# A gated linear scan over four batches: weight splits after a norm, other PSUM banks for two products, a third gate buffer

## The reference

```python
def _L0_attn_ref(x, W_in, conv_w, conv_b, W_g, b_g, forget_base, W_out):
    gx = jnp.einsum('ntd,hd->nth', x, W_in)
    gate, xb = (gx[..., :H], gx[..., H:])
    xb = _depthwise_causal_conv(xb, conv_w, conv_b)          # 4 taps along the tokens
    fg = jnp.einsum('nth,gh->ntg', xb, W_g) + b_g
    forget, inp = (fg[..., :H], fg[..., H:])
    alpha = jnp.exp(-8.0 * softplus(forget_base) * sigmoid(forget))
    beta = jnp.sqrt(1.0 - alpha ** 2 + 1e-6)
    h = _linear_scan(alpha, beta * sigmoid(inp) * xb)        # h[t] = alpha[t] h[t-1] + xs[t]
    return jnp.einsum('nth,dh->ntd', gelu(gate) * h, W_out)
x = x + _L0_attn_ref(_layernorm(x), ...)
```

## Time and profile before

| What | us |
|---|---|
| median of 3 timed runs (lowest, highest) | 990.32 (987.42, 992.02) |
| profiled execution, first to last instruction | 990.8 |
| PE busy, in the span | 924.9 (93%) |
| DVE, ACT, POOL busy | 675.9, 513.9, 422.6 |
| from the start to the end of the scan layer's pipeline on TensorE | about 131 |

### The profile page before, as it was taken

How to read it: one execution, slowest core, us unless ns; L and a number is a source line. 1 busy time by engine, 2 the same in 40 slices (tenths; PEclk the granted TensorE clock), 3 DMA queues, 4 the chain that set the end, 5 groups by cost and what they waited for, 6 DMA issues and landing times.

```text
span 990.8 us, 17519 instructions
## 1 busy us (share of the span) xinstructions
PE 924.9 (93%) x5688; PEld 774.2 (78%) x5688; DVE 675.9 (68%) x1706; ACT 513.9 (52%) x1221; POOL 422.6 (43%) x420
## 2 busy tenths in 40 slices
PE   5889996999999988999999899999999999889998
PEld 4668875787878866888888678887888888778887
DVE  6878797558687677677767555567766667735563
ACT  5467751313131426767666644454766666654443
POOL 5333354112221357767676400006776767631110
PEclk9889998999999999999999999999999999999999
DMA  7200123000000000000001030000000000000001
GB/s 261 70 1 16 48 65 112 1 1 0 0 0 1 1 23 1 2 23 0 22 0 33 12 105 15 4 25 2 2 24 0 22 0 12 27 15 17 31 25 46
DMA packets 15716, 26.34 MB, mean 27 GB/s; under 512 B 1642, under 2 KB 12256, under 8 KB 14896
## 3 DMA queue, kind: packets, MB, share of 16 engines
q1 hardware_dynamic: 15664, 25.69, 8.0%
HBM read 20.53 MB, written 2.10 MB: 23 GB/s over the span
## 4 chain that ended last, share of the span: by engine, by line
PE 72%; DVE 11%; ACT 6%; issue 3%; POOL 3%; SPq 3%; DMA 2%; ACTq 0%; DVEq 0%; POOLq 0%
PE bank L1593 33%; PE bank L1941 5%; PE bank L1895 5%; PE bank L1919 5%; PE bank L1801 5%; PE bank L1905 4%; ACT probs L1460 3%; PE bank L1764 2%; PE bank L1882 2%; PE bank L1747 1%; SPq L352 1%; DVE y L820 1%; PE bank L1929 1%; PE bank L2014 1%; PE bank L2011 1%
## 5 line engine op out<-in xcount | busy, mean ns | idle before, releaser
L1460 ACT ACTIVATE probs<-bank,row_min 128x256 f32<-128x256 f32 (+1 forms) x256 | 110.4, 458 | 120.1 <-DVE row_min L1048 120.1
L569 POOL TENSOR_TENSOR norms<-norms,minus_half 128x16 f32<-128x16 f32 x32 | 93.6, 2924 | 2.7
L1048 DVE CUSTOM_DVE_ANT_0 bank<-bank,mask 128x256 f32<-128x256 f32 (+1 forms) x256 | 90.7, 425 | 5.9 <-PE bank L1895 5.7
L1593 PE MATMUL bank<-wqkv_hi,x_hi 128*128 128x512 f32 x192 | 82.4, 429 | 1.8 <-DVE rot L1024 1.1
L1593 PE MATMUL bank<-wqkv_lo,x_hi 128*128 128x512 f32 x192 | 76.3, 397 | 0.0
L1593 PE MATMUL bank<-wqkv_hi,x_lo 128*128 128x512 f32 x192 | 75.7, 394 | 0.0
L1185 DVE SCALAR_TENSOR_TENSOR hidden<-bank,lcols,hidden 128x512 f32<-128x512 f32 (+1 forms) x48 | 36.0, 749 | 51.9 <-PE bank L1593 28.2
L551 POOL TENSOR_TENSOR q_tok<-rot 128x512 f32<-128x512 f32 x32 | 41.2, 1288 | 57.7 <-DVE rot L1024 57.7
L1905 PE MATMUL bank<-ident,probs 128*128 128x128 f32 x448 | 61.5, 279 | 3.9 <-ACT probs L1460 3.9
L1593 PE MATMUL bank<-t_hi,wm_hi 128*128 128x512 f32 x160 | 63.6, 397 | 0.0
L1593 PE MATMUL bank<-t_lo,wm_hi 128*128 128x512 f32 x160 | 63.5, 397 | 0.0
(11 more groups left out here) (253 smaller groups left out, 2639.5 us busy)
## 6 DMA issues: line engine op xcount, KB each, us to landing
w_stage<-in_wm_l_dram SPq DMA_DIRECT2D x8, 534.0 KB, 3.7
w_stage<-in_wqkv_dram SPq DMA_DIRECT2D x2, 1536.0 KB, 8.0
out_dram<-stream SPq DMA_DIRECT2D x8, 256.0 KB, 2.4
emb<-in_ctx_dram SPq DMA_DIRECT2D x1, 1536.0 KB, 6.8
inner<-in_w_gate_dram SPq DMA_DIRECT2D x1, 1152.0 KB, 10.3
stream<-in_x_dram SPq DMA_DIRECT2D x2, 512.0 KB, 5.7
stream<-in_x_dram SPq DMA_DIRECT2D x1, 1024.0 KB, 12.8
ew<-in_pos_bias_dram SPq DMA_DIRECT2D x1, 1024.0 KB, 11.5
```

The costliest lines, as they stand in the source:

```text
L569: pool.tensor_tensor(norms[:, 2, :], norms[:, 1, :], minus_half[:, :], ALU.pow).then_inc(c_rn, 1)
L1048: dve.tensor_tensor_reduce(logits, logits, mask[:, 2 * P - nk:2 * P], 1.0, FAR, ALU.add, ALU.min, row_min[:, w % 2, 2 * i + e:2 * i + e + ...
L1460: act.activation(probs[:, i, e, 0:nk], logits, ACT.Exp, bias=row_min[:, w % 2, h:h + 1], scale=-1.0, accum_out=row_sum[:, w % 2, h:h + 1]) ...
L1593: ins = pe.matmul(out, stationary, moving, start=(first and i == 0), stop=(last and i == len(terms) - 1))
```

## The change

Five edits, all in the scan layer.

- Gelu of batch 2 writes a third buffer, `gate_third`, which lies where later weights (`w_1_hi`) go; only batch 3 waits for a buffer, and that wait is for batch 0's products.
- Input products 5 and 6 of a batch go to banks 6 and 7, the output's. Their waits change with it: in batch 1 and 2 for Gelu of the batch before, in batch 3 for the residual of batch 0. The output waits for Gelu. The other four input products and all gate products go round banks 2 to 5, two banks further with each batch.
- On DVE, the residual of batch b - 1 stands in front of the scan of batch b (for b = 1 and 2), where it stood behind it.
- On GpSimd, batch 1's `rstd_of` stands directly after the first rounding of a gate weight, and the first subtraction waits until batch 1's norm has been applied; five of the six weight instructions then follow.
- On DVE, batch 1's norm is applied ahead of four small instructions on constants, and its `low_part` ahead of the second convolution instead of behind it.

```diff
@@ -131,6 +131,9 @@
         ew = sb("ew", [P, TT, T], stack=st_bias)
         st_bias.close()
         w_1_lo = sb("w_1_lo", [P, KD, FH], F32R, stack=st12)
+        st_third = ExitStack()
+        gate_third = sb("gate_third", [P, KR, T], stack=st_third)
+        st_third.close()
         w_1_hi = sb("w_1_hi", [P, KD, FH], F32R, stack=st12)
         w_2 = sb("w_2", [P, KF, D], stack=st12)
         rows = sb("rows", [P, 4, D], stack=st12)
@@ -259,6 +262,16 @@
         (a_in, x1_in) = signals("a_in x1_in")
         w_raw = inner[:, :, :].rearrange("p n d -> p (n d)")
 
+        gate_acts = (gate_act[:, 0, :, :], gate_act[:, 1, :, :], gate_third, gate_act[:, 0, :, :])
+
+        def input_bank(b, j):
+
+            return bank[2 + (j + 2 * max(b - 1, 0)) % 4] if j < 4 else bank[2 + j]
+
+        def gate_bank(b, u):
+
+            return bank[2 + (u + 2 * b) % 4]
+
         C_ZERO = 2
         tiles = lambda b: bass.ts(b, TT) if not isinstance(b, int) else slice(b * TT, (b + 1) * TT)
         block = ctx.enter_context(nc.Block())
@@ -424,17 +437,18 @@
                 pool.wait_ge(a_gelu, 3 * b + 3)
                 for j in range(KR):
                     pool.wait_ge(a_scan, 3 * b + j + 1)
-                    pool.tensor_tensor(scanned[:, j, :], scanned[:, j, :], gate_act[:, b % 2, j, :], ALU.mult)\
+                    pool.tensor_tensor(scanned[:, j, :], scanned[:, j, :], gate_acts[b][:, j, :], ALU.mult)\
                         .then_inc(a_gh, 1)
 
             pool.memset(beyond_raw[:, :], 0.0).then_inc(e_beyond, 1)
             rstd_of(0)
             pool.wait_ge(wg_in, 16)
             for k in range(KR):
-                if k == 1:
-                    rstd_of(1)
                 raw_k = w_raw[:, WIN_COLS + k * 2 * RH:WIN_COLS + (k + 1) * 2 * RH]
                 pool.tensor_scalar(w_gate_hi[:, k, :], raw_k, 1.0, 0.0, ALU.mult, ALU.add).then_inc(wg_hi, 1)
+                if k == 0:
+                    rstd_of(1)
+                    pool.wait_ge(n_norm, 2 * TT)
                 pool.wait_ge(wg_hi, k + 1)
                 pool.tensor_tensor(w_gate_lo[:, k, :], raw_k, w_gate_hi[:, k, :].bitcast(F32), ALU.subtract)\
                     .then_inc(wg_split, 1)
@@ -736,7 +750,9 @@
                 for j in range(KR):
                     dve.wait_ge(a_xs0, 3 * b + j + 1)
                     dve.tensor_tensor(th_in[:, j, :], th_in[:, j, :], beta[:, j, :], ALU.mult).then_inc(a_xs, 1)
-                if not (isinstance(b, int) and b == 0):
+                if 0 < b < NB - 1:
+                    residual(b - 1)
+                elif b:
                     dve.wait_ge(a_o, 2 * b)
                 for j in range(KR):
                     dve.wait_ge(a_xs, 3 * b + j + 1)
...
@@ -881,6 +897,7 @@
             dve.wait_ge(x1_in, 16)
             dve.wait_ge(a_tp, 2)
             norm_stats(1, 1)
+            norm_apply(1, 1, False)
             dve.wait_ge(col_in, 16)
             dve.tensor_scalar(fb_tmp[:, 2, :], cols[:, C_FB:C_FB + KR], 0.0, None, ALU.max).then_inc(fb_vec, 1)
             dve.tensor_scalar(half_bf[:, :], cols[:, C_BG:C_BG + 2 * KR], 0.5, None, ALU.mult).then_inc(fb_vec, 1)
@@ -889,10 +906,9 @@
             dve.tensor_tensor(fb_tmp[:, 2, :], fb_tmp[:, 2, :], fb_tmp[:, 0, :], ALU.add).then_inc(fb_vec, 1)
             dve.wait_ge(fb_vec, 3)
             dve.tensor_scalar(m4sp[:, :], fb_tmp[:, 2, :], -4.0, None, ALU.mult).then_inc(fb_vec, 1)
-            norm_apply(1, 1, False)
             conv_taps(0, 0)
+            low_part(1, a_tp_out, a_tp_lo)
             conv_taps(0, 1)
-            low_part(1, a_tp_out, a_tp_lo)
             conv_low(0, 0)
             conv_taps(0, 2)
             conv_low(0, 1)
@@ -921,9 +937,7 @@
                 for j in range(KR):
                     conv_low(b + 1, j)
                 recurrence(b)
-                if b:
-                    residual(b - 1)
-                else:
+                if b == 0:
                     largest_bias()
 
             for b in range(NB - 1):
...
@@ -1275,11 +1289,11 @@
 
             def gelu_gate(b):
 
-                if b > 1:
-                    act.wait_ge(a_gh, 3 * b - 3)
+                if b == NB - 1:
+                    act.wait_ge(a_gh, 3)
                 for j in range(KR):
                     act.wait_ge(a_in, 6 * b + KR + j + 1)
-                    act.activation(gate_act[:, b % 2, j, :], bank[2 + (KR + j) % 4][:, :], ACT.Gelu).then_inc(a_gelu, 1)
+                    act.activation(gate_acts[b][:, j, :], input_bank(b, KR + j)[:, :], ACT.Gelu).then_inc(a_gelu, 1)
 
 
             act.wait_ge(w1s_in, 16)
...
@@ -1608,17 +1622,17 @@
                 pe.wait_ge(a_tp_lo, 2 * b + 2)
                 for j in range(2 * KR):
                     m = (j + KR) % (2 * KR)
-                    if b == 1 and j < 2:
-                        pe.wait_ge(a_gelu, 2 + j)
-                    elif b == 1 and j < 4:
-                        pe.wait_ge((a_tap0, a_gelu)[j - 2], (3, 1)[j - 2])
+                    if b == 1:
+                        pe.wait_ge(a_tap0 if j < KR else a_gelu, j % KR + 1)
                     elif b and j < 4:
                         pe.wait_ge((a_thf, a_th)[j % 2], 3 * (b - 2) + (2 + j) // 2 + 1)
-                    if j >= 4:
-                        pe.wait_ge(a_tap0, 3 * b + j - 4 + 1)
+                    elif b == 2:
+                        pe.wait_ge(a_gelu, 3 + j - KR + 1)
+                    elif b:
+                        pe.wait_ge(a_res, 2 * (b - 3) + j - 4 + 1)
                     if b == 0 and j % KR == 0:
                         pe.wait_ge(win_lo, KD * (j // KR + 1))
-                    product(bank[2 + j % 4][:, :], [
+                    product(input_bank(b, j)[:, :], [
                         (w[:, k, m * P:(m + 1) * P], x[:, k, :]) for k in range(KD)
                         for w, x in ((w_in_hi, t_hi), (w_in_hi, t_lo), (w_in_lo, t_hi))]).then_inc(a_in, 1)
 
@@ -1629,11 +1643,11 @@
                         u = 2 * j + g
 
                         if b == NB - 1 and u < 4:
-                            pe.wait_ge((a_thf, a_th)[g], 3 * b - (0 if u < 2 else 1))
-                        elif u == 0:
-                            pe.wait_ge(a_tap0, 3 * (b + 1) + 3)
-                        elif u < 4:
-                            pe.wait_ge(a_gelu, 3 * (b + 1) + u)
+                            pe.wait_ge((a_thf, a_th)[g], 3 * b - (1 if u < 2 else 0))
+                        elif u < KR:
+                            pe.wait_ge(a_tap0, 3 * (b + 1) + u + 1)
+                        elif u == KR:
+                            pe.wait_ge(a_gelu, 3 * (b + 1) + 1)
                         elif u == 4:
                             pe.wait_ge(a_thf, 3 * b + 1)
                         else:
...
@@ -1653,6 +1667,7 @@
             def output(b):
 
                 pe.wait_ge(a_gh, 3 * b + 3)
+                pe.wait_ge(a_gelu, 3 * min(b + 3, NB))
                 pe.wait_ge(a_res, 2 * b)
                 for t in range(TT):
                     for k in range(KR):
```

More of the change, by code:

```diff
@@ L749, in recurrence @@
                     dve.wait_ge(a_scan, 3 * b + j + 1)
-                    dve.tensor_tensor(scanned[:, j, :], scanned[:, j, :], gate_act[:, b % 2, j, :], ALU.mult)\
+                    dve.tensor_tensor(scanned[:, j, :], scanned[:, j, :], gate_acts[b][:, j, :], ALU.mult)\
                         .then_inc(a_gh, 1)
@@ L1267, in taps @@
                 for j in range(KR):
-                    src = bank[2 + j % 4]
+                    src = input_bank(b, j)
                     act.wait_ge(a_in, 6 * b + j + 1)
@@ L1644, in gates @@
                                 pe.wait_ge(a_conv_lo, 3 * b + k + 1)
-                            ins = product(bank[2 + (u + 2) % 4][:, :], [
+                            ins = product(gate_bank(b, u)[:, :], [
                                 (w[:, k, m * P:(m + 1) * P], c[:, k, :])
```

4 lines of the change are left out of this document (2 added, 2 removed).

## The result

The changed kernel takes 981.59 us (median of 4 runs, 981.32 to 983.12) beside 991.17 of the kernel before in the same session; the ratio is 0.9915, 95% interval 0.9894 to 0.9936. Forecast were 986.8 us and a range of 982 to 990.5: the two medians lie 9.6 us apart (8.4 us by the ratio), not 3.5, and the time is 0.4 us under the lower end of the range. Run once more in another session it took 982.95 us (6 runs, 982.11 to 983.55), ratio 0.9924 [0.9904, 0.9945]. The profiled executions span 979.5 and 981.4 us, against 990.8.

What follows compares the result with a forecast made beforehand. TensorE was taken as the bound, through scan-layer waits and a slow clock. Banks and buffer 5.2 + first wait 1.1 - residual 0.8 - clock 2.0 = 3.5 us, from 990.32 to 986.8 us; range 982 to 990.5.

Steps and rivals of the forecast that it cites:

- What bounds it, and which waits go and come: TensorE bounds the kernel; its scan-layer waits go, a hidden 2.40 us norm wait appears, the rest moves as a block.
- The three waits: TensorE's waits: 4.8 us before batch 1's input products, 1.50 at batch 2's fifth, 2.95 at batch 1's second gate product.
- Banks and buffer, 5.2 us: Batch 2's input products to batch 3's transposes: second and third waits go, 7.63 us less a 2.40 us norm wait.
- The clock at the new wait, 2.0 us lost: Behind batch 3's transposes: TensorE's clock falls after the 2.40 us norm wait, costing 2.0 us, bounds nothing and 2.67.
- the case that the clock holds: Rival at batch 3's norm wait: the clock stays up, 5.5 us gained, 984.8 us; chance 0.26.
- The first wait, 1.1 us: Before batch 1's input products: earlier norm starts them at 27.9 instead of 28.95; bounds 3.4 gain to 0.5 loss.
- the first constant slips in, three constants and a tap go between: DVE instructions alternate with GpSimd's five weight instructions, which end at 25.3; the third tap ends at 26.6.
- so the slow stretch behind it stays: Behind batch 1's first input product: the idle ahead stays above 4 us, so TensorE's clock still falls.
- The residual, 0.8 us: Batch 3's gate products: the moved residual delays scan 2 and the tanh, losing 0.8 us; bounds nothing and 1.25.
- The row of 0.51 at 135.20: Next layer's transposes: after 1.7 us idle, clock 0.51 for 3.50 us, pricing the new wait's fall at 1.64.
- with the clock held, 982.5: Rival: DVE's taps slip between GpSimd's weight instructions (chance 0.15) and the clock also holds at the norm: 982.5 us.
- it would be wrong if batch 1's products started near 25.5: Sign against the prediction: batch 1's first input product near 25.5 on TensorE, where 27.5 to 28.2 was forecast.

Runs made afterwards that it cites:

- banks_buffer_alone: Changed kernel with the edits to batch 1's norm, `rstd_of` and `low_part` undone; banks, third buffer and residual's place stay changed: 986.92 us, ratio 0.9974.
- first profile: Profiled execution of the changed kernel in the first session, unedited; its span is 979.5 us.
- old_banks: Changed kernel with the banks of before and their waits; third buffer, residual and norm as changed: 982.76 us, ratio 0.9937.
- two_buffers: Changed kernel with two buffers for Gelu instead of three: 984.51 us, ratio 0.9946.
- three_more_small: Changed kernel with three more small 128x1 instructions on constants on DVE behind the four, results not used: 985.76 us (1 run) beside 990.83 before.
- second profile: Profiled execution of the unedited changed kernel run once more in another session; its span is 981.4 us, that session's median 982.95 us.
- bias_later_res_behind: Changed kernel with DVE's `largest_bias` moved from before batch 3's norm into batch 2, and batch 1's residual back behind batch 2's scan: 979.79 us, ratio 0.9887.

## Why the prediction was right and wrong

- **What bounds it, and which waits go and come.** Right. The three waits were the ones, the wait for the norm came in their place, no residual was waited for, and the rest moved as a block but for the clock.
- **Banks and buffer, 5.2 us.** Right in size: 5.17, 5.16 (banks_buffer_alone) and 5.78, and right in its mechanism: batch 3's norm, 32.73 us behind batch 0's first gate product, is what TensorE then waits for. The 5.78 belongs to the first profile, where batch 0's gate products, and so its scan and batch 3's norm, came 2.04 us earlier than in the second (34.34 against 36.38), but batch 2's products only 1.43. What the prediction did not see is that the two edits do not add: the buffer alone gives 5.16 (old_banks) and the ring alone 5.83 (two_buffers), since either leaves TensorE at the norm's wait.
- **The clock at the new wait, 2.0 us lost.** This step failed. "I take that the clock falls" was put between 1.50 (up) and 2.95 (down), with 1.7 before transposes as the nearest row. All runs with waits up to 3.25 us at this place show 1.00, and the stretch behind batch 3's transposes lost 0.05 us instead of 2.0. Putting the idles in order of length was the wrong tool; the case that the clock holds had been given 0.26.
- **The first wait, 1.1 us.** The mechanism held, the step "the first constant slips in, three constants and a tap go between" failed by two turns: a second constant slipped in ahead of the first subtraction and the first tap ahead of the second. three_more_small takes the tap's turn away again and lands at 27.52 beside the forecast 27.9. So the term was mis-sized: the product came 2.6 us (second profile) and 3.1 us (first) earlier instead of 1.1. The sentence "so the slow stretch behind it stays" came true in the second profile, where the 36 input products of batch 1 take 10.05 us beside 10.23 before, and was wrong in the first, where they take 8.47; of the 1.76 us won there 0.46 come back as the wait for batch 2's `t_lo`. The Trainium skill (SBUF — State Buffer, Who interferes with whom) states that the order of issue, not the kind of operation, decides who blocks. The traces agree: 20.37 before 20.52 against 20.45 behind 20.42. One pair in the earlier trace rows fits less well: the norm started at 18.21, 0.02 us ahead of the subtraction, and was the one held.
- **The residual, 0.8 us.** Right: 0.76 lost behind batch 3's gates, 0.60 of it a wait for the tanh, and it goes when that residual goes back (20.73 us from batch 3's gate products to the scan end in bias_later_res_behind, as in the kernel before).
- **Not in the sum: 1.5 us behind the scan layer.** The row of 0.51 at 135.20 was used for a price only. The wait ahead of it is as long as before (1.59 against 1.7), but the clock stayed at 1.00. That it would move with the program wasn't asked. As the same idle there left the clock up in some traces and let it fall in others, no run here ties these 1.5 us to the change.
- **Of the rivals**, the sentence "with the clock held, 982.5" names what came: taps that slip in and a clock that holds at the norm. Its gain of 7.8 us lies between the 7.1 and 9.2 us of the two scan ends; that the whole time comes so near is part luck, since another 2.1 or 2.3 us come from behind the scan layer. The prediction itself wrote that it would be wrong if batch 1's products started near 25.5, and they did, at 25.87.

What stays open is why the clock falls behind one idle of 1.7 and not behind another of 3.25, nor, at one place, behind 1.59 in one trace and not in another. No run here tells more than that length and place don't say it.

## What to carry to other kernels

Where a trace shows instructions of two engines holding each other up, write down the starts to a hundredth of a microsecond and count the turns: a few tenths of a microsecond of small instructions can move everything behind by a turn, so give the bounds of such a term at least the weight of the middle. Before adding up two removed waits, ask which wait is the next to show: where it comes first, one of the two edits may be enough. And a clock seen slow behind an idle is a fact of that run; price it as a chance, in both directions, and look for slow stretches later in the program that may go too.
